# A two-layer transformer on one Trainium2 core: layer-0 experts computed on each token's two picks, through rows laid out by expert in DRAM

## What is computed

```python
# layer 0, experts (E = 8, K = 2, inner width 128), x is [4096, 128]
logits = x @ router_weight
top_vals, top_idx = top_k(logits, K)
w = zeros((T, E)).at[arange(T)[:, None], top_idx].set(softmax(top_vals))
gu = einsum('th,ehf->tef', x, gate_up_proj) + gate_up_proj_bias
gate, up = minimum(gu[..., ::2], 7.0), clip(gu[..., 1::2], -7.0, 7.0)
act = (up + 1.0) * gate * sigmoid(gate * 1.702)
down = einsum('tei,eih->teh', act, down_proj) + down_proj_bias
x = layernorm(x + einsum('te,teh->th', w, down))
# layer 1, attention, its first step
q, k, v = x @ Wq.T, x @ Wk.T, x @ Wv.T
```

## Time and profile before

| | |
|---|---|
| median of 3 runs | 874.67 us (871.64 to 878.95) |
| the profiled execution's own time | 872.83 us |
| its span (first to last instruction) | 871.1 us |
| PE busy | 677.3 us, 78% |
| DVE busy | 560.3 us, 64% |
| POOL busy | 506.0 us, 58% |
| ACT busy | 464.6 us, 53% |
| mean granted TensorE clock | 0.9 of full |

### The profile page before, as it was taken

How to read it: one execution, slowest core, us unless ns; L and a number is a source line. 1 busy time by engine, 2 the same in 40 slices (tenths; PEclk the granted TensorE clock), 3 DMA queues, 4 the chain that set the end, 5 groups by cost and what they waited for, 6 DMA issues and landing times. The chain is left out here.

```text
span 871.1 us, 18432 instructions
## 1 busy us (share of the span) xinstructions
PE 677.3 (78%) x6663; PEld 420.5 (48%) x6663; DVE 560.3 (64%) x1476; ACT 464.6 (53%) x690; POOL 506.0 (58%) x652
## 2 busy tenths in 40 slices
PE   7747999999768999999986767999996513898400
PEld 3423555555435566666653434766664202555300
DVE  5877888888377977787787662444546884122116
ACT  5434777777655666666654674667663600232102
POOL 7844777767553555555554784666663602787743
PEclk9976999999989999999997996999998755899765
DMA  5764473431000000000002799999990350355344
GB/s 159 245 212 95 126 192 101 120 85 42 3 2 1 1 2 1 1 1 1 1 2 78 235 287 184 199 194 189 186 196 12 107 137 13 75 122 100 34 88 126
DMA packets 134984, 86.04 MB, mean 99 GB/s; under 512 B 11120, under 2 KB 131440, under 8 KB 134768
## 3 DMA queue, kind: packets, MB, share of 16 engines
q1 hardware_dynamic: 128112, 79.57, 38.6%
q0 software_dynamic: 5632, 4.33, 3.8%
q10 hardware_dynamic: 1152, 0.98, 0.4%
HBM read 54.96 MB, written 29.49 MB: 97 GB/s over the span
## 5 line engine op out<-in xcount | busy, mean ns | idle before, releaser
L771 POOL TENSOR_TENSOR m_prod<-m_upc,m_gatec 128x512 f32<-128x512 f32 x64 | 99.5, 1555 | 101.9 <-DVE m_upc L601 101.9
L2161 ACT ACTIVATE a_prob<-a_ps_pair 128x1024 f32<-128x1024 f32 x96 | 93.1, 1024 | 48.2 <-PE a_ps_pair L1997 36.3
L2173 POOL TENSOR_SCALAR_AFFINE_SELECT a_prob<-a_prob 128x512 f32<-128x512 f32 (+1 forms) x96 | 76.5, 804 | 51.1 <-ACT a_prob L2161 50.9
L1832 ACT ACTIVATE a_prob<-a_ps_pair 128x1024 f32<-128x1024 f32 x96 | 96.6, 1024 | 13.2 <-PE a_ps_pair L1635 10.3
L1873 POOL TENSOR_SCALAR_AFFINE_SELECT a_prob<-a_prob 128x512 f32<-128x512 f32 (+1 forms) x96 | 75.5, 787 | 41.2 <-ACT a_prob L1832 40.5
L1771 DVE TENSOR_REDUCE a_mx<-a_ps_pair 128x4 f32<-128x1024 f32 x64 | 77.8, 1220 | 24.3 <-PE a_ps_pair L1676 22.6
L715 ACT ACTIVATE m_gate<-m_ps_g,bgu 128x512 f32<-128x512 f32 x64 | 44.0, 687 | 47.5 <-PE m_ps_g L460 47.5
L460 PE MATMUL m_ps_g<-m_x1T,wgu 128*128 128x512 f32 x128 | 66.2, 599 | 0.0
L1417 ACT ACTIVATE c_hT<-c_ps_x,c_w 128x512 f32<-128x512 f32 x16 | 11.0, 688 | 102.2 <-PE c_ps_x L1236 102.2
L462 PE MATMUL m_ps_u<-m_x1T,wgu 128*128 128x512 f32 x128 | 65.4, 592 | 0.0
L1450 POOL DMA_INDIRECT sum<-c_o,c_idx x32 | 50.4, 1574 | 16.5 <-issue 8.5
(11 more groups left out here) (297 smaller groups left out, 1696.9 us busy)
## 6 DMA issues: line engine op xcount, KB each, us to landing
qst<-scratch_q SPq DMA_DIRECT2D x64, 128.0 KB, 4.0
kst<-scratch_k SPq DMA_DIRECT2D x64, 128.0 KB, 3.9
scratch_q<-p_parts SPq DMA_DIRECT2D x16, 384.0 KB, 2.8
scratch_k<-p_parts SPq DMA_DIRECT2D x16, 384.0 KB, 2.8
qst<-scratch_q SPq DMA_DIRECT2D x32, 192.0 KB, 5.4
kst<-scratch_k SPq DMA_DIRECT2D x32, 192.0 KB, 5.3
c_w<-in_w SPq DMA_DIRECT2D x8, 578.0 KB, 3.9
scratch_q<-parts SPq DMA_DIRECT2D x16, 256.0 KB, 2.5
```

Source lines behind the costliest of these rows:

```text
L771: nc.gpsimd.tensor_tensor(prod[:, n % 2, :], upc[:, n % 2, :], gatec[:, n % 2, :], ALU.mult).then_inc(s_pr, 1)
L1832: nc.scalar.activation(prob[:, r % 6, :], pair[(0, 2, 1)[j]][:, :], ACT.Exp, scale=scale, bias=0.0).then_inc(s_e, 1)
L2161: nc.scalar.activation(prob[:, r % 6, :], pair[r % 2][:, :], ACT.Square, scale=scale, bias=1.0).then_inc(s_e, 1)
L2173: nc.gpsimd.affine_select(out=blk, in_=blk, compare_op=ALU.is_ge, fill=0.0, base=0, pattern=[[0, n], [1, P]], channel_multiplier=-1).then_ ...
```

## The change

`expert_layer0` and `project_layer1` are replaced by one block, `picked_experts`. Each half of the tokens (16 tiles, 2048 tokens, 4096 picks) is treated alike:

- The router's scores come straight out as [tokens, experts] (`logits`). DVE marks the two picks, PE counts them by expert with two matmuls against a triangular and a ones matrix (`prefix`), and DVE turns the counts into a row number for each pick (`place_picks`): rows of one expert stand together, each expert begins at a multiple of 512 rows, and a half has 15 such units of 512 rows (`NUNIT`), each of one expert.
- POOL scatters each normalised tile twice, once for each pick, into a DRAM array `picked` (64 indirect DMAs of 128 rows in all, `scatter`). The arrays have been filled with zeros by 30 DMAs of 256 KB from SP in the attention of layer 0.
- 30 units follow. SP loads a unit's 512 rows (`load`, four buffers), PE turns them, ACT copies them, the expert's gate and up weights are fetched by a register-indexed ACT copy (`take_weights`), PE expands; DVE clips out of PSUM and makes product and activation (four instructions of 512 columns); PE adds the down bias by one bf16 matmul and the four down matmuls, ACT copies the result (`copy_out`) and SP stores it to a DRAM array `downs` (`store`).
- POOL gathers the results back, 8 indirect DMAs per chunk, when all stores of a half have landed; DVE adds the two of each token with their weights (`add_picks`, 8 instructions per chunk), takes statistics and inverts the spread.
- The projection of layer 1 stands in the same block. Residuals are formed by PE (it subtracts the parts in PSUM with matmuls against minus the identity), the high and middle parts by ACT, the low part by DVE. For chunks 4 to 7 the adding of picks stands between the projections of two chunks.
- The list of later weights has 23 arrays instead of 20.

The instruction order of SP, PE, ACT and DVE in the units:

```diff
+XIN, WBUFS, OBUFS, GBUFS = 4, 3, 3, 4
+COMBINE_AT = (21, 24, 27)
+NUNIT = (2 * P * HALF + E * (UNIT - 1)) // UNIT
             @block.sync
+                def load(n):
+                    if n % NUNIT == 0:
+                        sp.wait_ge(s_sc[n // NUNIT], 32 * HALF)
+                    after(sp, s_up, n - XIN + 1)
+                    sp.dma_start(xin[:, n % XIN, :], unit_rows(picked, n)).then_inc(s_xin[n % XIN], 16)
+                def store(n):
+                    sp.wait_ge(s_ob, n + 1)
+                    sp.dma_start(unit_rows(done_d, n), ob[:, n % OBUFS, :]).then_inc(s_ost[n % OBUFS], 16)
+                for n in range(NU2 + XIN - 1):
+                    if n < NU2:
+                        load(n)
+                    if n >= XIN - 1:
+                        store(n - XIN + 1)
...
             @block.tensor
+                turn_unit(0)
+                for n in range(NU2):
+                    if n + 1 < NU2:
+                        turn_unit(n + 1)
+                    expand(n)
+                    if n >= 2:
+                        reduce(n - 2)
+                reduce(NU2 - 2)
+                turn_next(0)
+                reduce(NU2 - 1)
...
+                def reduce(n):
...
+                    after(pe, s_ob, n - 1)
+                    e = pe.value_load(expert[0:1, n:n + 1], min_val=0, max_val=E - 1)
+                    nc.tensor.matmul(ps_d[n % 2][:, :], sel[:, bass.ds(e, 1), :].bitcast(BF16), bdq[:, :, :],
+                                     start=True, stop=False, skip_group_check=True)
+                    pe.wait_ge(s_act, n + 1)
+                    for j in range(4):
+                        here = slice(j * P, (j + 1) * P)
+                        last = nc.tensor.matmul(ps_d[n % 2][:, here], act[:, n % 2, here], wd[:, bass.ds(e, 1), :],
+                                                start=False, stop=True, skip_group_check=True)
+                    last.then_inc(s_dn, 1)
...
             @block.scalar
+                for n in range(NU2):
+                    if n + 1 < NU2:
+                        copy_unit(n + 1)
+                    tanh(n)
+                    if n + WBUFS - 1 < NU2:
+                        take_weights(n + WBUFS - 1)
+                    if n >= 2:
+                        copy_out(n - 2)
...
             @block.vector
+                for n in range(NU2):
+                    clip_gate(n)
+                    if n > 0:
+                        activate(n - 1)
+                    clip_up(n)
+                    multiply(n)
+                    if n in COMBINE_AT:
+                        add_picks(COMBINE_AT.index(n))
```

The projection of a chunk c:

```diff
             @block.tensor
+                    project(c, 0)
+                    project(c, 1)
+                    less_hi(c, 0)
+                    project(c, 2)
+                    less_hi(c, 1)
+                    project(c, 3)
+                    less_mid(c, 0)
+                    less_hi(c, 2)
+                    if c + 1 < NCH:
+                        turn_next(c + 1)
+                    less_mid(c, 1)
+                    less_hi(c, 3)
+                    project_v(c)
+                    less_mid(c, 2)
+                    less_mid(c, 3)
...
             @block.scalar
+                    hi(c, 3)
+                    mid(c, 2)
+                    mid(c, 3)
+                    if 4 <= c + 2 < NCH:
+                        normalise_next(c + 2)
...
             @block.vector
+                    for i in range(4):
+                        lo(c, i)
+                    keep_v(c)
+                    if 4 <= c + 2 < NCH:
+                        add_picks(c + 2)
+                        row_stats(c + 2)
+                        merge_rows(c + 2)
+                        invert(c + 2, c + 3)
+                        normalise_next(c + 2)
...
             @block.gpsimd
+                scatter(0)
+                scatter(1)
+                nc.gpsimd.memset(v_all[:, :, :, HD:HV], 1.0).then_inc(s_ones, 1)
+                stored(NUNIT)
+                for c in range(4):
+                    gather(c)
+                stored(2 * NUNIT)
+                for c in range(4, NCH):
+                    gather(c)
```

In the attention of layer 0, on SP, ahead of the `later` loads of a step:

```diff
+                    if 1 <= u <= 2 * NUNIT:
+                        if u == 1:
+                            sp.wait_ge(s_empty, 1)
+                        rows_of = picked[(u - 1) // NUNIT][UNIT * ((u - 1) % NUNIT):UNIT * ((u - 1) % NUNIT) + UNIT, :]
+                        sp.dma_start(rows_of.rearrange("(p j) c -> p (j c)", j=4), empty[:, :]).then_inc(s_clear, 16)
```

More of the change, by code:

```diff
@@ L354, in expert_layer0 @@
+        wqk, wv = consts["later"]["wqk1"], consts["later"]["wv1"]
+        bdr = sb("bdr", [P, C])
         bdp = sb("bdp", [P, 3, C], BF16)
[L355 to L363, removed]
@@ new lines, in prefix, with turn_unit @@
+                def prefix(h):
+                    pe.wait_ge(s_sel, h + 1)
+                    for i, left in enumerate((upper, ones_sq)):
+                        last = nc.tensor.matmul(ps_u[h][:, P * i:P * i + P], left[:, :], both[:, h, :, :].rearrange("p t e -> p (t e)"),
+                                                start=True, stop=True)
+                    last.then_inc(s_pre, 1)
+                def turn_unit(n):
+                    pe.wait_ge(s_xin[n % XIN], 16 * (n // XIN) + 16)
+                    if n < 2:
+                        pe.wait_ge(s_xT, NCH)
+                    after(pe, s_ux, n - 1)
+                    for j in range(4):
+                        last = nc.tensor.transpose(ps_x[n % 2][:, j * P:(j + 1) * P], xin[:, n % XIN, j * P:(j + 1) * P], ident[:, :])
+                    last.then_inc(s_up, 1)
@@ L924, in _, with keep_v @@
+                def keep_v(c):
                     ve.wait_ge(s_vp, c + 1)
@@ L927, in _ @@
                                           ps_v[:, :].rearrange("p (t h d) -> p t h d", t=4, h=H)).then_inc(s_vc, 1)
-            @block.scalar
-            def _(act):
-                def copy_x(c):
-                    act.wait_ge(s_xp, c + 1)
-                    after(act, s_vp, c - 1)
-                    nc.scalar.activation(x2T[:, c % 2, :], ps_x[c % 2][:, :], ACT.Copy).then_inc(s_xT, 1)
+                for c in range(2):
+                    normalise(c)
+                make_shift(slice(0, norm.early))
@@ new lines, in _ @@
+                for c in range(2, 5):
+                    normalise(c)
+                norm.invert_rest(ve, s_inv)
+                make_shift(slice(norm.early, NTILE))
+                for c in range(5, NCH):
+                    normalise(c)
+                nc.vector.memset(ones8[:, :], 1.0).then_inc(s_rt, 1)
+                done[0] += 1
+                mark_picks(0)
+                place_picks(0)
+                mark_picks(1)
+                for col, scale, add in ((1, -1.0, LIMIT), (2, -1.0, -LIMIT), (3, 1.0, 1.0)):
+                    here = wall[:, :, 2 * P + col]
+                    nc.vector.tensor_scalar(here, here, scale, add, ALU.mult, ALU.add).then_inc(s_bnd, 1)
@@ L945, in _ @@
+                    nc.scalar.activation(part(c, i, 1), ps_qk[i][:, :], ACT.Copy).then_inc(s_mid, 1)
+                for c in range(4):
+                    normalise(c)
                 copy_x(0)
+                for c in range(1, NCH):
+                    if c + 3 < NCH:
+                        normalise(c + 3)
+                    copy_x(c)
+                runner_up(0)
+                runner_up(1)
+                for n in range(WBUFS - 1):
+                    take_weights(n)
+                copy_unit(0)
```

909 lines of the change are left out of this document (424 added, 485 removed).

## The result

The changed kernel takes 1059.89 us (median of 4 runs, 1058.93 to 1061.48) against 876.25 us for the kernel before, measured beside it: a ratio of 1.210, 95% interval 1.205 to 1.216. The forecast was 1016 us, with a range of 950 to 1090. The direction and the mechanism came out as foretold; the ring through SP's queue cost more than foretold, and so did the attention and the routing.

A forecast was written before the change was run, and what follows sets the result against it. PE bounds the old experts, a chunk-to-chunk chain the projection; the new units wait on SP's load-store ring. Terms 16.5 + 46 + 13 + 239 + 6 + 98 + 4 replace 283.3; with attention +2, 1016 us, range 950 to 1090.

The forecast's parts named there:

- the ring through SP's queue: Units from unit 4 on: load n+1 stands behind store n-3, so no load is hidden; 9.2 us each, 239 us.
- attention of layer 0: SP's 33 added DMA issues there cause lag, mostly covered by the lead of two steps: 2 us, bounds 0 and 14.
- routing: Before the scatters: DVE normalises, marks and places the picks, with matmuls between; first row numbers after 16.5 us.
- scatter, landing, load 0: Before the units: 32 scatters of 1.25 us on POOL, a landing of 2.6 and load 0 with 3.4; 46 us.
- first iterations: Start of the units: three iterations without the ring, cold and filling the pipe; 13 us.
- rings and last unit: Units: 26 rings of 9.2 us, 239 us, then the last unit's expand, clip, tanh, activation and reduces, 6 us.
- projection, tail, border: Behind the units: chunk chains 62, adding picks 32, clock 4, together 98 us; tail and border of blocks 4 us.
- Rival A: Units: the closed ring through SP's queue holds as forecast; 1016 us, own range 960 to 1075, chance 0.75.
- B: Units: loads are issued early enough that PE never waits and sets the pace; 869 us, chance 0.08.
- clock term: Rings: idle PE makes some start at half speed; 0.8 us put on the mean ring.
- Rival C: Units: every burst runs at half clock, rings of 11.85 us; 69 us more, 1085 us, chance 0.12.
- D: Scatter costs what scatter-add costs and SP bounds the attention: 20 + 12 us more, 1048 us, chance 0.05.

The follow-up runs named there:

- the repeat: The changed kernel measured a second time with nothing altered, in another session: 1131.17 us, ratio 1.282 to the kernel before.
- the last run: Against the 878.91 us kernel with all repairs and spaced indirect DMAs: chunks 4 to 7 turned at chunk end, first 8 second-half scatters unspaced; 857.70 us, ratio 0.980.

## Why the forecast was right, and where it was off

The steps in the order of the sum, forecast against the profile of the result (own time 1061.48 against 1014):

| step | forecast | measured |
|---|---|---|
| attention of layer 0 | +2 | +13.4 (243.8 to 257.2) |
| routing | 16.5 | 27.2 (to 284.4) |
| scatter, landing, load 0 | 46 | 44.4 (to 328.8) |
| first iterations | 13 | 15.4 (to 344.2) |
| rings and last unit | 239 + 6 | 256.3 (25 periods) + 13.0 (to 613.5) |
| projection, tail, border | 98 + 4 | 103.4 |

The steps miss by 48 us in all, and nearly all of it one way: 24 in the rings and the last unit, 11 in the attention, 11 in the routing. No large errors cancelled; the range of 140 us was wide enough. The first transposes of a loaded unit, foretold for about 306 us, came at 328.8.

**The mechanism was right.** Rival A's ring is in the timeline as its own steps name it, and the run with later stores takes it away and leaves 3.26 us a unit. So B's condition (loads issued early enough) was rightly judged false for this order of SP, and its pace of 3.7 us rightly judged reachable.

**The ring was mis-sized in its clock term.** Outside PE I had 4.65 us, and 4.1 were measured: the load landed after 2.9 us, not 3.4. The leg at full clock was too dear as well: 7.3 us for the ring with PE kept busy, where the forecast had 8.4 before the clock. The clock, put at 0.8 us as a mean, costs 2.9. That 7.3 lies at the forecast's own lower bound, 7.4, which took full clock and a landing of 2.5. The errors partly cancel: 9.2 against 10.25, or 27 us over 26 rings. Rival C had the clock right (every burst starts at half clock) and the sum wrong, since it took the whole PE leg at half speed and the 4.65. I had read the rows as an idle PE that keeps its clock for some us; in the rings of the result every gate ran at the lower one, after waits of 3.7 to 4.9 us; in the repeat two bursts began at the full one.

That each burst behind a DMA wait starts at the lower clock is what the Trainium skill, "TensorE: Matmul & The Clock Gate", section "HAM oscillation — how this bites in real kernels", says, and the run that fills the wait agrees: 0.67 becomes 1.00. By the Trainium skill, "DMA: Bandwidth & Descriptors", section "Anatomy of one DMA — SWDGE (gpsimd) path", 256 KB would land after an estimated 2.6 us, but its figures are for DMAs issued from GpSimd and these come from SP's queue. The loads took 2.9 us and the stores, of the same size, 2.0; the 3.4 that I took came from the loads of `xc`.

**The attention was off by nearly its upper bound.** A stretch of more than 5 us was one of the forecast's own signs of being wrong, and it came: 13.4 us. I wrote that the lead of two steps would cover most of 8 us of lag. It covered nothing that shows. My reading, which no run isolates: a lead is used up once, and a lag that grows with each pair is paid in full. The bound of 14 was the better forecast. The run with the clears on POOL's queue gives 10 of it back.

**The routing was off by the order on PE.** I counted DVE's steps and left out that PE turns and scores eight chunks at half clock, 2.45 us each, and that the count of the first half stood behind all of them. Moving it gives 4.2 us; the rest I put down to the scoring itself, which no run isolates.

**The projection was right** in its total and in its parts: 8.5 us of wait four times against 7.9 forecast.

D fell: a scatter is issued in 0.99 us and 0.30 of gap, close to the gather of the earlier trace rows and not to the scatter-add. Its second half, SP as the bound of the attention, did come true, with 13 us.

**What the forecast could not see** is the wait beside POOL's bursts. It is absent in the profile of the result, whose four times agree within 0.3%, and costs 71 us in the repeat. Shown: it comes with indirect DMAs 1.25 us apart, all but goes when they are 1.57 us apart and where POOL is silent (what is left is 3 us or less a time), takes ACT and DVE alike, and is always a wait for PE. PE itself went on: in the run with PE kept busy its gate matmuls ended at 503.66 by the model and 12 later ones had been started by 509.6, while DVE's clip of that gate came at 523.31. Not shown: what in the chip holds the word from PE back, and why the runs of the result and the last run were spared. All nine profiles without the spacing had it on three chips, and the fourth chip, which ran the last kernel alone, did not; the profile has no row that names the cause.

## What to carry to other kernels

In a queue that holds both loads and stores, write down for each load what the store ahead of it waits for: buffers are worth nothing if the load that fills them stands behind a store of the same round, and moving the stores two places in the queue was worth some 150 us here. The rings here left PE waiting some 4 us and cost the wait and, on top, 2.9 us for the lower clock in the burst behind it; filling the wait with useless matmuls is a cheap way to measure which part is which. Repeat the unaltered kernel beside its variants: the same program moved by 71 us here between two measurements, and two good edits looked like nothing until their stages were read by themselves.

## What was not expected of the hardware

- Beside back-to-back indirect DMAs on POOL (0.95 us each, 0.30 between), ACT and DVE can stand idle for up to 24 us after the matmuls that they wait for have ended by the profile; 0.3 us more between the DMAs removes nearly all of it. The pauses of POOL are paid back many times: 72 us between two kernels that differ in nothing else. Two of the five sessions did not show it: that of the result, and that of the last run, where even unspaced gathers had no such wait.
- The kernel before, which has such bursts only near its end, moved by 1% over all measurements (873.8 to 881.2 us), the changed one by 7%.
- A 256 KB load from DRAM landed after 2.9 us in the median and a store of the same shape after 2.0; a zero fill from one buffer to DRAM after 2.6, beside the attention's traffic, and the same fill issued from POOL after 3.7.
- PE was granted 0.50 through the whole of the routing (258 to 284), though its row has it busy for 21 of the 26 us, with transposes and scores.
